# Pairs 5, 8 and 11 of x turned wholly by the tensor engine, in a fused attention and FFN block

## What is computed

```python
xn = layernorm(x)
s = xn @ Win + bin_                       # 512 -> 64
h = relu(s[..., None] * W1 + b1)          # 64 -> 64 x 16
g = (h * W2).sum(-1) + b2                 # -> 64
ffn = g @ Wout + bout                     # 64 -> 512
att = attention(xn)                       # three rounds; see below
out = x + att + ffn
```

## Time and profile before

| | before |
|---|---|
| median of 3 runs | 306.65 us (306.26 to 307.37) |
| the profiled execution, its time | 306.89 us |
| its span, first to last instruction | 305.1 us |
| busy: PE / DVE / POOL / ACT | 91% / 80% / 77% / 74% |
| PE chain share of the span | 64% (DVE 20%) |

### The profile page before, as it was taken

The page is one execution under the profiler, slowest core; times in us unless marked ns, Lnnn a source line. Parts: engine busy times, 40 slices in busy tenths (PEclk is TensorE's granted clock), DMA queues, the critical chain, the costliest instruction groups (busy, mean ns, idle before and its releaser), DMA issues.

```text
span 305.1 us, 6171 instructions
## 1 busy us (share of the span) xinstructions
PE 277.8 (91%) x2363; PEld 115.9 (38%) x2363; DVE 244.5 (80%) x383; ACT 224.5 (74%) x264; POOL 234.0 (77%) x209
## 2 busy tenths in 40 slices
PE   4797598979999999999999999999989999998881
PEld 4652356424343434335343535343432433331120
DVE  0779475999997899996899978899999999924354
ACT  1546734964889699897979698989759789897800
POOL 8533019999498997979895969979793989899900
PEclk9999699997999999999999999999999999999798
DMA  7999979998978799999799999999799999335467
GB/s 235 294 370 380 282 166 337 365 298 295 306 267 238 252 356 308 371 297 383 176 371 248 393 289 305 330 336 353 186 388 269 399 264 290 150 127 230 103 230 281
DMA packets 50573, 87.87 MB, mean 288 GB/s; under 512 B 6360, under 2 KB 35184, under 8 KB 46448
## 3 DMA queue, kind: packets, MB, share of 16 engines
q1 hardware_dynamic: 46400, 65.96, 69.5%
q10 hardware_dynamic: 3504, 21.37, 19.9%
q0 software_dynamic: 640, 0.16, 0.9%
HBM read 53.77 MB, written 33.69 MB: 287 GB/s over the span
## 4 chain that ended last, share of the span: by engine, by line
PE 64%; DVE 20%; issue 5%; POOL 3%; DMA 3%; ACT 3%; DVEq 0%; POOLq 0%; ACTq 0%
PE sg L530 14%; PE sg L564 14%; PE op L593 13%; DVE x L1001 6%; PE ra L548 4%; DVE stats L1024 4%; DMA b2c<-in_L_ffn_b_dram 3%; PE ra L593 3%; ACT H L772 2%; DVE xqT L1011 2%; PE op L345 2%; PE rb L476 2%; PE op L476 1%; PE ra L476 1%; PE ra L345 1%
## 5 line engine op out<-in xcount | busy, mean ns | idle before, releaser
L1148 POOL TENSOR_TENSOR x<-x,bias_row 128x512 f32<-128x512 f32 x128 | 160.5, 1293 | 0.0
L1024 DVE BATCH_NORM_STATS2 stats<-x 128x6 f32<-128x512 f32 x128 | 80.7, 672 | 8.9 <-DMA x<-in_L_attn_x_dram 8.9
L1001 DVE TENSOR_TENSOR x<-x,op 128x1024 f32<-128x1024 f32 x48 | 58.2, 1213 | 27.1 <-PE op L593 27.0
L772 ACT ACTIVATE H<-ra,b1c,w1c 128x1024 f32<-128x1024 f32 x64 | 72.8, 1206 | 7.9 <-PE rb L548 7.8
L772 ACT ACTIVATE H<-rb,b1c,w1c 128x1024 f32<-128x1024 f32 x64 | 73.4, 1223 | 3.3 <-PE sg L564 3.3
L564 PE MATMUL sg<-H,w2s 128*32 128x512 f32 x512 | 65.4, 623 | 2.9 <-ACT H L772 2.9
L593 PE MATMUL op<-wout,G 64*128 64x512 f32 x192 | 54.8, 648 | 5.5 <-DVE x L1001 3.2
L1132 POOL TENSOR_TENSOR rstd<-veps,nhalf 128x8 f32<-128x8 f32 x16 | 26.7, 1671 | 42.8 <-DVE veps L1036 42.7
L530 PE MATMUL sg<-xT,win 128*32 128x512 f32 x256 | 58.0, 595 | 1.3 <-ACT xqT L747 0.9
L530 PE MATMUL sg<-xqT,winq 128*32 128x512 f32 x224 | 50.8, 595 | 0.0
L1011 DVE STREAM_TRANSPOSE xqT<-xq 128x1024 f32<-128x1024 f32 x28 | 34.5, 1234 | 1.2 <-DMA xq<-in_L_attn_x_dram 1.2
(11 more groups left out here) (191 smaller groups left out, 340.1 us busy)
## 6 DMA issues: line engine op xcount, KB each, us to landing
out_dram<-x SPq DMA_DIRECT2D x30, 1024.0 KB, 6.5
x<-in_L_attn_x_dram ACTq DMA_DIRECT2D x10, 2048.0 KB, 10.5
xq<-in_L_attn_x_dram SPq DMA_DIRECT2D x112, 128.0 KB, 6.0
x<-in_L_attn_x_dram SPq DMA_DIRECT2D x12, 1024.0 KB, 11.8
out_dram<-x SPq DMA_DIRECT2D x4, 512.0 KB, 4.0
x<-in_L_attn_Wq_dram SPq DMA_DIRECT2D x1, 1024.0 KB, 18.0
x<-in_L_attn_Wk_dram SPq DMA_DIRECT2D x1, 1024.0 KB, 20.0
x<-in_L_attn_Wv_dram SPq DMA_DIRECT2D x1, 1024.0 KB, 8.2
```

The costliest lines, as they stand in the source:

```text
L772: act.activation(Hr[half][k % len(Hr[half])][:, :], rep_ps[half][:, :], ACT.Relu, bias=b1c[:, half, k:k + 1], scale=w1c[:, half, k:k + 1]) ...
L1001: dve.tensor_tensor(both, both, sum_banks(n, j)[:, :].rearrange("p (h d) -> p h d", h=2), ALU.add).then_inc(add_done, 1)
L1024: dve.bn_stats(stats[:, j, :], x_sb[m][:, j * D:(j + 1) * D]).then_inc(bn_done, 1)
L1148: pool.tensor_tensor(x_sb[m][:, c], x_sb[m][:, c], bias_row[:, :], ALU.add).then_inc(xc_done, 1)
```

## The change

Three pairs, 5, 8 and 11 (WHOLE), have their half 1 turned as half 0 is. For them `load_quads` and `turn_quads` do nothing. PE gets `turn(n, 2)` and `turn(n, 3)`, both into RA and both one step early, in step n - 1; ACT gets `evacuate(n, 2)` behind `relu(n - 2, 5)` and `evacuate(n, 3)` behind `relu(n - 2, 7)`, into xT1, and `s_product` reads xT1 with the weights win. Since RA is in use, in steps 4, 7 and 10 `project(n - 2, 2)` goes to o_ps and stands between the two `sum_h`, and `turn(n, 0)` of the three pairs waits for `evacuate(n, 3)`. The places of some attention parts move by up to a step. (Before, QUADS is all pairs from 2 on.)

```diff
@@ -188,20 +188,22 @@
         TILES = TPP // 2
         LAST = N - 1
         BY_PE = 2
+        WHOLE = (5, 8, 11)
+        QUADS = [n for n in range(BY_PE, N) if n not in WHOLE]
         BIAS_ORDER = (0, 4, 1, 5, 2, 6, 3, 7)
         AT_PE = iter((
             -32, 10, 13, 13, 13, 13, 13, 15, 15, 15, 16, 16, 16, 16, 16, 16, 16, 16, 16, 66, 69, 71, 75, 99,
-            102, 106, 130, 134, 137, 163, 166, 196, 198, 201, 224, 228, 230, 235, 260, 266, 288, 291, 294,
-            297, 320, 324, 326, 357, 358, 363, 386,))
+            102, 106, 130, 134, 137, 162, 166, 197, 198, 202, 224, 228, 230, 232, 235, 262, 265, 288, 291,
+            294, 297, 323, 326, 356, 358, 384, 388,))
         AT_ACT = iter((
-            10, 18, 18, 18, 18, 18, 18, 18, 18, 18, 66, 107, 107, 130, 137, 160, 160, 164, 171, 196, 203,
-            203, 225, 228, 233, 233, 257, 263, 266, 291, 292, 296, 298, 321, 321, 324, 352, 357, 361, 386,))
+            10, 18, 18, 18, 18, 18, 18, 18, 18, 18, 66, 107, 107, 130, 137, 139, 139, 163, 192, 197, 203,
+            203, 225, 228, 232, 232, 234, 259, 264, 289, 290, 291, 296, 320, 320, 324, 331, 356, 363, 389,))
         AT_DVE = iter((
             -32, -32, 2, 2, 4, 5, 7, 8, 8, 8, 16, 17, 18, 21, 22, 22, 22, 22, 22, 22, 69, 75, 79, 98, 105,
-            164, 164, 170, 171, 174, 175, 201, 239, 240, 260, 260, 265, 266, 273, 324, 324, 330, 331, 336,
-            337, 362, 363, 366,))
+            164, 164, 170, 171, 176, 177, 202, 235, 237, 240, 242, 260, 261, 269, 324, 324, 330, 330, 336,
+            338, 362, 363, 367,))
         AT_POOL = iter((
-            0, 0, 103, 136, 168, 230, 262, 321, 352,))
+            0, 0, 103, 136, 192, 230, 261, 296, 328,))
 
         def reach(steps, n, place):
 
@@ -246,13 +248,15 @@
 
             return (ld[n][h], 16) if n < RING else (ldp[n % RING], 16 * (n // RING))
 
-        def load_quads(k):
-
-            r, n, h = k % 3, k // 2 + BY_PE, k % 2
+        def load_quads(n, h):
+
+            if n not in QUADS:
+                return
+            k = 2 * QUADS.index(n) + h
             if k > 2:
                 sp.wait_ge(tq_done, k - 2)
             for i in range(DC):
-                sp.dma_start(xq[r][i * QD:(i + 1) * QD, :], xq_v[n, 2 + h, i, :, :]).then_inc(ldq[r], 16)
+                sp.dma_start(xq[k % 3][i * QD:(i + 1) * QD, :], xq_v[n, 2 + h, i, :, :]).then_inc(ldq[k % 3], 16)
 
         def load_weight(i, w):
             sp.dma_start(w_nat[i], w.rearrange("(c p) i -> p c i", p=P)).then_inc(in_w[i], 16)
@@ -279,8 +283,8 @@
...
+            load_quads(2, 0)
+            load_quads(2, 1)
...
@@ -295,19 +299,17 @@
                 sp.dma_start(scal[:, i:i + 1], v.partition_broadcast(P)).then_inc(in_scal, 16)
             load(3, 0)
             load(3, 1)
-            load_quads(2)
-            load_quads(3)
+            load_quads(3, 0)
+            load_quads(3, 1)
             load(4, 0)
             load(4, 1)
             load(5, 0)
             load(5, 1)
             for n in range(2, N + 2):
-                if has(n + 2):
-                    load_quads(2 * (n + 2 - BY_PE))
+                load_quads(n + 2, 0)
                 store(n - 2, 0)
                 store(n - 2, 1)
-                if has(n + 2):
-                    load_quads(2 * (n + 2 - BY_PE) + 1)
+                load_quads(n + 2, 1)
 
 
         def product_qk():
@@ -442,7 +444,11 @@
 
         def groups(n):
 
-            return 2 * DC * min(n, BY_PE) + DC // 2 * max(0, n - BY_PE)
+            return 2 * DC * min(n, BY_PE) + DC // 2 * max(0, n - BY_PE) + DC // 2 * sum(m < n for m in WHOLE)
+
+        def place_of(n, i):
+
+            return groups(n) + ((i + 2) % 4 if n in WHOLE else i)
 
         def first_bank(n, g):
 
@@ -481,16 +487,23 @@
             m = n % RING
             if i == 0:
                 pe.wait_ge(*(landed(n, 0)))
-                if has(n - 3):
+                if n in WHOLE:
+                    pe.wait_ge(ev_done, place_of(n, 0))
+                elif has(n - 3):
                     pe.wait_ge(add_done, TILES * (n - 3) + 3)
                 else:
                     pe.wait_ge(turn_dve, 2 * DC)
                     pe.wait_ge(turn_act, 2 * DC)
+            elif i == 1:
+                pe.wait_ge(relu_done, TPP * (n - 1))
+            elif i == 2:
+                pe.wait_ge(*(landed(n, 1)))
+                pe.wait_ge(relu_done, TPP * (n - 2) + HK)
             else:
-                pe.wait_ge(relu_done, TPP * (n - 1))
+                pe.wait_ge(ev_done, place_of(n, 3))
             for k in range(2):
-                c = 2 * i + k
-                mm = turn_halves(quarter_banks(rep_ps[i])[:, :, k, :], lambda j: x_sb[m][:, j * D + c * P:j * D + (c + 1) * P])
+                c = i // 2 * HALF + (2 * (i % 2) + k) * P
+                mm = turn_halves(quarter_banks(rep_ps[i == 1])[:, :, k, :], lambda j: x_sb[m][:, j * D + c:j * D + c + P])
             mm.then_inc(tr_done, 1)
 
         def rstd_banks():
@@ -512,7 +525,7 @@
                 pe.wait_ge(s_done, 1)
             else:
                 pe.wait_ge(g_made, n - 1)
-                pe.wait_ge(tq_done, 2 * (n + 1 - BY_PE))
+                pe.wait_ge(tq_done, 2 * sum(m <= n for m in QUADS))
             if n == BY_PE:
                 pe.wait_ge(win_centred, 2)
             pe.wait_ge(ev_done, groups(n + 1))
@@ -522,7 +535,7 @@
                         own = sg_ps[b * M + a * MH:b * M + (a + 1) * MH, :]
                         if b == 0:
                             w, turned_x = win, xT[:, c, :]
-                        elif n < BY_PE:
+                        elif n not in QUADS:
                             w, turned_x = win, xT1[:, c, :]
                         else:
                             w, turned_x = winq, xqT[:, :, c, :]
@@ -566,9 +579,13 @@
                                    tile_position=(0, at0))
             mm.then_inc(g_done, 1)
 
+        def in_ra(n):
+
+            return n < N - 2 and n + 3 not in WHOLE
+
         def sum_banks(n, j):
 
-            if j == 2 and n < N - 2:
+            if j == 2 and in_ra(n):
                 return RA_ps
             return {(LAST, 1): RA_ps, (LAST, 2): RB_ps}.get((n, j), o_ps)
 
@@ -582,12 +599,12 @@
                     pe.wait_ge(R_done, n + 3)
                 else:
                     pe.wait_ge(add_done, TILES * n)
-            elif j == 2 and n < N - 2:
+            elif j == 2 and in_ra(n):
                 pe.wait_ge(relu_done, TPP * (n + 1) + HK)
             elif n == LAST and j < 3:
                 pe.wait_ge(relu_done, TPP * N)
             else:
-                pe.wait_ge(add_done, TILES * n + {1: 1, 2: 2, 3: 1 if n == LAST else 2 if n < N - 2 else 3}[j])
+                pe.wait_ge(add_done, TILES * n + {1: 1, 2: 2, 3: 1 if n == LAST else 2 if in_ra(n) else 3}[j])
             for b in range(2):
                 own = slice(b * M, (b + 1) * M)
                 mm = pe.matmul(sum_banks(n, j)[:, b * D:(b + 1) * D], G[n % 2][own, j * P:(j + 1) * P], wout[own, :],
@@ -651,14 +668,25 @@
                 reach(side, n, 5)
                 s_product(n)
                 reach(side, n, 6)
+                if n + 1 in WHOLE:
+                    turn(n + 1, 2)
                 project(n - 2, 1)
                 reach(side, n, 7)
-                project(n - 2, 2)
-                reach(side, n, 8)
-                sum_h(n - 1, 0)
-                reach(side, n, 9)
-                sum_h(n - 1, 1)
-                reach(side, n, 10)
+                if n + 1 in WHOLE:
+                    sum_h(n - 1, 0)
+                    reach(side, n, 8)
+                    project(n - 2, 2)
+                    reach(side, n, 9)
+                    sum_h(n - 1, 1)
+                    reach(side, n, 10)
+                    turn(n + 1, 3)
+                else:
+                    project(n - 2, 2)
+                    reach(side, n, 8)
+                    sum_h(n - 1, 0)
+                    reach(side, n, 9)
+                    sum_h(n - 1, 1)
+                    reach(side, n, 10)
                 project(n - 2, 3)
                 reach(side, n, 11)
             replicate(LAST)
@@ -747,9 +775,10 @@
             act.activation((xT if b == 0 else xT1)[:, c, :], first_bank(n, g), ACT.Copy).then_inc(ev_done, 1)
 
         def evacuate(n, i):
-            act.wait_ge(tr_done, groups(n) + i + 1)
+            act.wait_ge(tr_done, place_of(n, i) + 1)
             act.wait_ge(sc_done, DC * n)
-            act.activation(xT[:, 2 * i:2 * i + 2, :].rearrange("p c (h x) -> p h c x", h=2), quarter_banks(rep_ps[i]), ACT.Copy).then_inc(ev_done, 1)
+            act.activation((xT1 if i > 1 else xT)[:, i % 2 * 2:i % 2 * 2 + 2, :].rearrange("p c (h x) -> p h c x", h=2),
+                           quarter_banks(rep_ps[i == 1]), ACT.Copy).then_inc(ev_done, 1)
 
         def copy_rstd(n):
             act.wait_ge(rb_done, n + 1)
@@ -828,6 +857,8 @@
                     if r == 6 and n + AHEAD >= RING and has(n + AHEAD):
```

(10 more changed lines are left out.)

## The result

The changed kernel takes 311.0 us (median of 4 runs, 308.48 to 311.82) against 306.72 us: ratio 1.0143, 95% interval 1.0108 to 1.0177. It is slower by 1.4%; I had forecast 310.9 us.

A forecast was written before the change was run, and what follows sets the result against it. The prediction took PE's own work to set every step's length. PE work +4.7, new waits +0.5 and +0.5, old waits given back -1.5 make +4.2 us: 311.1 us profiled, 310.9 us median, range 307.3 to 312.9 us.

The forecast's parts named there:

- the stretch: From step 3's replicate to step 15's, where the whole change lies: forecast 4.2 us longer.
- PE's busy time: Steps 4, 7 and 10: lone turns, the moved project and separated sum_h add 4.7 us of PE work.
- new waits: PE waits for DVE's add and for evacuate(n, 3) in the steps with new turns: 1.0 us together.
- old waits given back: Steps 5, 8, 11 and 12: DVE's lighter load shortens PE's waits by 1.5 us, at most 2.48.
- The waits for the add: project(n - 2, 2) on o_ps waits about 0.25 us for add(n - 2, 1), covered in step 7: 0.5 us.
- Those for the evacuation: turn(n, 0) waits for evacuate(n, 3): about 0.1 us in steps 4 and 10, 0.3 in step 7, sum 0.5.
- 0.8 us wait for the last attention part: Steps 11 and 12: PE's wait for DVE shrinks to about 0.5 us as that part moves behind replicate.
- its signs of being wrong: PE busy under 2.5 us more, a plain step off 13.77 us, or about 1 us wait before turn(n, 0).
- A: Steps with attention: DVE's chain sets the pace, so its relief gives 2.9 us back, 303.8 us; chance 7%.
- B: No change: cheap turns of 0.98 us a pair, no new waits, nearly all idle time goes, 307.2 us; chance 12%.
- C: Steps 4, 7 and 10: late evacuate(n, 3) makes turn(n, 0) wait the whole 1.02 us, 313.4 us; chance 9%.
- D: Steps 4 to 12: one more stretch at half clock costs up to 1.7 us, 312.6 us; chance 2%.

The follow-up runs named there:

- experiment 3: The changed kernel with the attention parts at the places they had before the change: stretch 207.07 us, ratio 1.016.
- experiment 1: The kernel before, with half 1 of pairs 5, 8 and 11 neither read again nor transposed: 303.95 us against 306.22, ratio 0.993.
- experiment 6: The changed kernel with third project back on RA behind both sum_h, turn(n, 3) into RB, turn(n, 1) between the last two sum_h: stretch 205.93 us, ratio 1.0135.
- experiments 4 and 5: Change for pair 14 alone, old attention places: step 13 16.15 us against 13.77; kernel before, only step 13's third project on o_ps between both sum_h: 14.95 us.
- experiment 8: The kernel before, with half 0 of the last pair transposed by DVE in step 14 instead of turned by PE: 304.74 us against 306.36, ratio 0.9958.
- experiment 10: The kernel before without PE's two turns and ACT's evacuations of half 0 of pairs 5, 8 and 11: stretch 202.09 us, nothing gained.
- experiment 12: The kernel before without DVE's reads and transposes of half 1 and PE's turns of half 0 of pairs 5, 8 and 11: stretch 3.07 us shorter.

## Why the prediction was right

**The sum.** +4.2 us were forecast for the stretch and +4.20 measured. That agreement is luck: the errors of three terms (-1.05, +0.8 and +0.25 us) cancel.

| term | forecast | measured |
|---|---|---|
| PE's busy time | +4.7 | +3.65 |
| new waits | +1.0 | +1.8 |
| old waits given back | -1.5 | -1.25 |

Of the old waits 3.03 - 1.80 = 1.23 us are left, so 1.25 of 2.48 us are given back. The first term was nearly right for what it names: with the old places the three steps with the turns hold 4.6 us more of PE's work (experiment 3). In them a lone turn takes 0.64 to 0.71 us, a little over my 0.64, and the project behind it 0.94 us in place of 1.06. What I had left out lies elsewhere: the relief takes 0.5 us off PE's busy time (experiment 1), and so do the moved attention parts (203.71 against 203.25 us, experiment 3). The second was too small. The waits for the add (0.33 and 0.32 us, none in step 7) came out near the working. Those for the evacuation came to 0.6 us in place of 0.5, but not where I had them: 0.30 and 0.29 us in steps 4 and 10 (I had 0.1 each) and none in step 7 (I had 0.3). And in step 10 `turn(11, 2)` waits 0.6 us for the relus that free RA. I had called that wait the one that `project(n - 2, 2)` had at the same place. It isn't the same place: the turn stands ahead of `project(n - 2, 1)`, one project sooner, with four activations of the attention (L755, 1.70 us) among ACT's relus; in experiment 6, with the same attention places but the turn behind that project, PE doesn't wait there. In a step without attention the order alone costs half of the whole (experiments 4 and 5), against 0.6 in 1.9 us by my terms.

**The give-back.** The 0.8 us wait for the last attention part stayed at 0.8; I had it at 0.5. Step 5 gave back 1.1 us where I had at most 0.7; 0.75 us of it comes from the relief alone (15.11 us, experiment 1).

**The signs.** Two of those that the prediction named did not come: PE's idle time in the stretch is 3.03 us, not under 2.5, and steps 7 and 10 are 2.4 us longer, not at most 2.1. None of its signs of being wrong showed.

**What bounds the kernel.** This is the step that held only in part. That added work on PE costs at least its full length was right in every run that added some, and in the steps without attention PE is the bound both ways (0.99 us off for two turns less, experiment 8). But I took the small idle time of PE for proof that PE alone sets the steps with attention too. It isn't: there, less work on PE is worth nothing (experiment 10), since DVE is full in the step behind: before the change it is busy 15.72 of 15.86 us in step 5, 17.55 of 17.65 in step 8 and 18.45 of 18.69 in step 11. In each of the couples 4 and 5, 7 and 8, 10 and 11 DVE's chain ends about when PE's does, and only less work on both shortens them by much (experiment 12). The rule of the Trainium skill ("Perfetto Trace Analysis", "Identifying the Most-Contended Engine") that matmul busy time is a poor sign of how near TensorE is to its limit was nearer to this than I allowed: of DVE's relief, 0.54 us came out of PE's busy time. Its other half, to judge by the weight loads, this case doesn't bear out: in a step without attention PEld is busy 4.86 of 13.77 us, and still the two turns taken out of it shortened it by all of their 0.99 us.

**The rivals.** A (a gain of 2.9 us) failed: without any new turn the relief is worth 1.5 us. Under the load of the turns it is worth 2.2 us, and the load costs 6.4. B and C failed too; no new wait was longer than 0.6 us. B's 307.2 us lies just outside the stated range, which begins at 307.3, though B had a chance of 12%. D: the clock was full through the whole stretch.

## What to carry to other kernels

Work that moved here from the second busiest engine to the busiest one cost its full length and more, and gave back no more than the busiest had waited for the other: ask for both sides, and try the relief alone before building the move. Count the order too: a step that takes a PSUM bank for itself pushes its neighbours onto shared banks, and in the one step where it was tried alone that cost 1.2 us, as much as adding the turns. A small idle time of one engine shows that more work there will cost, not that less will help; for that, look at how full the next engine is in the step behind.

## What the runs showed that I had not expected

The same group of four `project` matmuls takes 0.86 us behind another project, 0.94 behind a turn, 1.06 behind `s_product` or `sum_h` and 1.13 to 1.15 after a wait, all of it counted as busy. A turn takes 0.49 us behind a project and 0.71 after a wait. So a wait costs 0.1 to 0.2 us more than the idle time that the profile shows, and two kernels with the same matmuls differ in PE's busy time (199.60 and 199.06 us, experiment 1).
